# Linear attention with routed experts on one core: the last steps in another order, and the last head of the last block projected by rows

## The reference, cut to what matters

```python
qkv = silu(xn @ w_qkv.T); q, k, v = split per head            # 16 heads of 128
# per head, by blocks of rows, with a state kv that decays:
o_inter = (q * q_decay) @ kv
o_intra = ((q @ k.T) * diag_decay) @ v
kv = block_decay * kv + (k * k_decay).T @ v
out = o_inter + o_intra                                        # all heads side by side: 2048 columns
var = mean(out * out, axis=-1)
out = norm_w * (out * rsqrt(var + EPS))
gate = sigmoid(xn @ w_gate.T)
attn = (gate * out) @ w_out.T                                  # back to 256 columns
result = x + attn + (routed experts + shared experts)(xn)
```

## Time and profile before

| | |
|---|---|
| median of 3 runs | 1753.86 us (1752.04 to 1755.01) |
| the profiled execution | 1752.27 us, its span 1750.5 us |
| granted TensorE clock, mean | 0.997 of full speed |
| TensorE busy | 1709.8 us (98%), weight loads 1513.5 us |
| VectorE busy | 1308.6 us (75%) |
| ScalarE, GpSimd busy | 720.2 us, 607.3 us |

### The profile page before, as it was taken

The page is one execution under the profiler, slowest core; times in us unless marked ns, Lnnn a source line. Parts: engine busy times, 40 slices in busy tenths (PEclk is TensorE's granted clock), DMA queues, the critical chain, the costliest instruction groups (busy, mean ns, idle before and its releaser), DMA issues.

```text
span 1750.5 us, 34484 instructions
## 1 busy us (share of the span) xinstructions
PE 1709.8 (98%) x11705; PEld 1513.5 (86%) x11705; DVE 1308.6 (75%) x2590; ACT 720.2 (41%) x1331; POOL 607.3 (35%) x826
## 2 busy tenths in 40 slices
PE   6999999999999999999999999999999999999997
PEld 5888899899988888888888888889999999999996
DVE  7888788888776676666667667668888888876666
ACT  4333443434344444444444444443434343434331
POOL 2333155555343333433333343333333323210011
PEclk9999999999999999999999999999999999999998
DMA  6666444344478888878888787854444444331234
GB/s 219 217 218 232 139 137 150 129 147 134 151 235 255 243 247 251 247 243 245 251 249 249 244 256 238 256 170 134 124 125 125 129 117 139 103 113 51 78 99 133
DMA packets 283501, 316.02 MB, mean 181 GB/s; under 512 B 37696, under 2 KB 233280, under 8 KB 283328
## 3 DMA queue, kind: packets, MB, share of 16 engines
q1 hardware_dynamic: 211008, 175.34, 32.7%
q0 software_dynamic: 33792, 88.13, 16.7%
q10 hardware_dynamic: 38528, 50.34, 8.1%
HBM read 169.21 MB, written 144.46 MB: 179 GB/s over the span
## 4 chain that ended last, share of the span: by engine, by line
PE 73%; DMA 12%; DVE 5%; POOL 4%; issue 4%; ACT 1%; SPq 0%; DVEq 0%; ACTq 0%; POOLq 0%
DMA rows_turned<-xz 12%; PE bank L1251 6%; PE bank L1293 6%; PE bank L1252 6%; PE bank L1253 6%; PE bank L1276 5%; PE bank L1231 5%; PE bank L1233 5%; PE bank L1232 5%; PE bank L1296 5%; PE bank L1284 5%; POOL xsT L582 4%; PE bank L1307 3%; PE bank L1305 3%; PE bank L1306 3%
## 5 line engine op out<-in xcount | busy, mean ns | idle before, releaser
L582 POOL DMA_DIRECT2D xsT<-rows_turned x384 | 210.3, 554 | 388.4 <-DMA rows_turned<-xz 378.3
L1251 PE MATMUL bank<-wh,xh 128*128 128x256 f32 x1024 | 293.9, 287 | 0.0
L1253 PE MATMUL bank<-wh,xl 128*128 128x256 f32 x1024 | 289.1, 282 | 0.0
L1252 PE MATMUL bank<-wl,xh 128*128 128x256 f32 x1024 | 288.9, 282 | 0.0
L680 ACT ACTIVATE kv<-bank 128x512 f32<-128x512 f32 x256 | 153.1, 598 | 224.4 <-PE bank L1253 224.4
L593 POOL DMA_INDIRECT yk<-slot_y,pos x128 | 131.7, 1029 | 260.5 <-DVE xr L1005 171.2
L1039 DVE STREAM_TRANSPOSE kz<-kv 128x512 f32<-128x512 f32 x127 | 90.2, 710 | 166.0 <-issue 149.0
L1251 PEld LDWEIGHTS bank<-wh,xh 128*128 128x128 f32 x1024 | 193.3, 189 | 19.2 <-issue 15.9
L1231 PE MATMUL bank<-xh,wh 128*128 128x512 f32 x512 | 208.9, 408 | 0.0
L1055 DVE SCALAR_TENSOR_TENSOR og<-tg,bank 128x512 f32<-128x512 f32 x128 | 88.0, 687 | 155.0 <-ACT o L706 155.0
L1293 PE MATMUL bank<-sm,kv 128*128 128x128 f32 x1024 | 197.9, 280 | 4.7 <-DVE sm L1019 4.4
(11 more groups left out here) (165 smaller groups left out, 3692.2 us busy)
## 6 DMA issues: line engine op xcount, KB each, us to landing
keys_turned<-kz SPq DMA_DIRECT2D x127, 256.0 KB, 2.9
kT_by_group<-keys_turned SPq DMA_DIRECT2D x508, 64.0 KB
slot_x<-zeros ACTq DMA_DIRECT2D x8, 3072.0 KB, 10.2
xs<-slot_x SPq DMA_DIRECT2D x96, 256.0 KB, 3.8
we<-wexp_in SPq DMA_DIRECT2D x192, 128.0 KB, 3.0
rows_turned<-xz POOLq DMA_DIRECT2D x96, 256.0 KB, 4.1
xsT<-rows_turned POOLq DMA_DIRECT2D x384, 64.0 KB, 3.0
slot_y<-ys ACTq DMA_DIRECT2D x96, 256.0 KB, 3.9
```

Of the source, the lines that this page charges most:

```text
L582: pool.dma_start(xsT[q % 2][b * TB:(b + 1) * TB, :, :, :].rearrange("p a k j -> p a (k j)"), xz_back[q % 2, b]).then_inc(xsT_loaded[q % 2] ...
L1251: pe.matmul(dst, lh, rh, start=(k == 0), stop=False)
L1252: pe.matmul(dst, lh, rl, start=False, stop=False)
L1253: mm = pe.matmul(dst, ll, rh, start=False, stop=(k == KD - 1))
```

## The change

- **Turns 122 to 127.** `squares` moves from the end of the turn to before `project_out(s-2, 1)`. `turn_back` moves up to the end of the same turn, before the next turn's keys' and values' projection. `last_sum` moves to the start of the next turn on VectorE, and `mean_squares` ahead of `low_og`.
- **After the loop.** The loops of TensorE and VectorE end at turn 127 and the rest is written out (SyncE's loop ends one turn earlier). `scores(127)` stands ahead of `project_out(126, 0)`. `project_out(126, 1)` writes bank 2, so that it needs not wait for the first half to be added. `squares(6)` goes to bank 3, `squares(7)` to bank 5.
- **Last block, last head.** `earlier_heads` turns block 7's `acc` as it stands after 15 heads, by fp32 matmuls against the identity, into banks 0 and 1, open for accumulation. `last_head` adds the last head's projection there, with `ogh` and `ogl` as the stationary operand, 256 output features wide: 12 matmuls of 128x256. `add_out(127, ...)` is gone.
- **Last step's gate.** `gate_o(127)` waits for bank 4 alone; ScalarE makes `ogh` first and squares afterwards.
- **Stores.** There are three `res` buffers in place of two (with their semaphores), and each block is stored in two halves of 256 KB, the first after two of the four sums.

```diff
@@ -447,26 +448,27 @@
             def load_last(b):
-                if b < 2:
+                if b < 3:
                     for r in range(2):
...
                 else:
-                    sp.wait_ge(out_stored[b % 2], 16 * (b // 2))
-                sp.dma_start(res[b % 2][:], part2_grp[b]).then_inc(res_loaded[b % 2], 16)
+                    sp.wait_ge(out_stored[b % 3], 32 * (b // 3))
+                sp.dma_start(res[b % 3][:], part2_grp[b]).then_inc(res_loaded[b % 3], 16)
...
             def store_last(b):
-                sp.wait_ge(final, CH * (b + 1))
-                sp.dma_start(out_grp[b], res[b % 2][:]).then_inc(out_stored[b % 2], 16)
+                for h in range(0, CH, 2):
+                    sp.wait_ge(final, CH * b + h + 2)
+                    sp.dma_start(out_grp[b][:, h:h + 2, :], res[b % 3][:, h:h + 2, :]).then_inc(out_stored[b % 3], 16)
...
                 load_head(1, part)
-            for s in range(SLOTS + 1):
+            for s in range(SLOTS):
                 q0 = 2 * (s - EXPERT0)
...
                     pair_done(q0 - 1)
-                if s > FIRST_OUT + 3:
-                    store_last(s - FIRST_OUT - 4)
+                if s > FIRST_OUT + 2:
+                    store_last(s - FIRST_OUT - 3)
                 if s == EXPERT0 - 2:
@@ -493,12 +495,12 @@
                 if s == FIRST_OUT:
-                    for b in range(2):
+                    for b in range(3):
                         load_last(b)
-                if FIRST_OUT + 4 <= s < FIRST_OUT + 2 + NSB:
-                    load_last(s - FIRST_OUT - 2)
-            for r in range(2):
-                sp.wait_ge(out_stored[r], 16 * NSB // 2)
+                if FIRST_OUT + 4 <= s < FIRST_OUT + 1 + NSB:
+                    load_last(s - FIRST_OUT - 1)
+            for r in range(3):
+                sp.wait_ge(out_stored[r], 32 * len(range(r, NSB, 3)))
@@ -702,6 +704,8 @@
                 act.wait_ge(o_mm, j + 1)
+                if j == NSTEP - 1:
+                    act.wait_ge(og_ready, j + 1)
                 act.wait_ge(ssq_added, j)
@@ -750,7 +754,10 @@
                     silu_pair(q0 + 1)
-                if attends:
+                if s == NSTEP:
+                    high_og(s - 1)
+                    square_o(s - 1)
+                elif attends:
                     square_o(s - 1)
@@ -1051,7 +1058,9 @@
                 dve.wait_ge(tanh_done, j + 1)
-                dve.wait_ge(o2_ready, j + 1)
+                dve.wait_ge(o_mm, j + 1)
+                if j < NSTEP - 1:
+                    dve.wait_ge(o2_ready, j + 1)
                 dve.scalar_tensor_tensor(og[:], tg[:], 1.0, bank[4][:], ALU.add, ALU.mult).then_inc(og_ready, 1)
@@ -1061,11 +1070,12 @@
                 a = acc[:, k, tok(d % NSB)]
+                src = bank[2 if (d, k) == (NSTEP - 2, 1) else 5][:]
                 if d < NSB:
-                    dve.tensor_copy(a, bank[5][:]).then_inc(acc_added, 1)
+                    dve.tensor_copy(a, src).then_inc(acc_added, 1)
                 else:
                     dve.wait_ge(acc_added, KD * (d - NSB) + k + 1)
-                    dve.tensor_tensor(a, a, bank[5][:], ALU.add).then_inc(acc_added, 1)
+                    dve.tensor_tensor(a, a, src, ALU.add).then_inc(acc_added, 1)
@@ -1080,19 +1090,23 @@
                 dve.wait_ge(rms_mm, b + 1)
-                dve.tensor_scalar(rmsv[:, b * CH:(b + 1) * CH], bank[6][:, 0:CH], 1.0 / (NH * HD), RMS_EPS,
+                src = bank[(3, 5)[b - NSB + 2] if b >= NSB - 2 else 6][:, 0:CH]
+                dve.tensor_scalar(rmsv[:, b * CH:(b + 1) * CH], src, 1.0 / (NH * HD), RMS_EPS,
                                   ALU.mult, ALU.add).then_inc(rmsv_ready, 1)
...
             def last_sum(b):
-                dve.wait_ge(accT_mm, b + 1)
+                if b < NSB - 1:
+                    dve.wait_ge(accT_mm, b + 1)
                 dve.wait_ge(rms_ready, b + 1)
-                dve.wait_ge(res_loaded[b % 2], 16 * (b // 2 + 1))
-                for c in range(CH):
-                    o = res[b % 2][:, c, :]
-                    src = bank[6 + c // 2][:, (c % 2) * D:(c % 2 + 1) * D]
+                dve.wait_ge(res_loaded[b % 3], 16 * (b // 3 + 1))
+                for c in range(CH):
+                    o = res[b % 3][:, c, :]
+                    if b == NSB - 1:
+                        dve.wait_ge(last_mm, c // 2 + 1)
+                    src = bank[(0 if b == NSB - 1 else 6) + c // 2][:, (c % 2) * D:(c % 2 + 1) * D]
                     dve.scalar_tensor_tensor(o, src, rms[:, b * CH + c:b * CH + c + 1], o, ALU.mult, ALU.add).then_inc(final, 1)
...
-            for s in range(SLOTS):
+            for s in range(NSTEP):
                 experts = EXPERT0 <= s < EXPERT1
@@ -1100,6 +1114,8 @@
                     add_squares(s - 2)
+                if s > FIRST_OUT + 2:
+                    last_sum(s - FIRST_OUT - 3)
                 if EXPERT0 <= s + 1 < EXPERT1:
@@ -1129,20 +1145,31 @@
                     decay_queries(s)
-                if s > FIRST_OUT + 2:
-                    last_sum(s - FIRST_OUT - 3)
                 if experts:
...
                     add_out(s - 2, 1)
+                if s >= FIRST_OUT + 2:
+                    mean_squares(s - FIRST_OUT - 2)
                 if attends:
...
                     routing(0)
-                if FIRST_OUT + 2 <= s < SLOTS - 1:
-                    mean_squares(s - FIRST_OUT - 2)
+            update_state(NSTEP - 1)
+            decay_scores(NSTEP - 1)
+            add_squares(NSTEP - 2)
+            last_sum(NSB - 3)
+            gate_o(NSTEP - 1)
+            add_out(NSTEP - 2, 0)
+            low_og(NSTEP - 1)
+            add_squares(NSTEP - 1)
+            add_out(NSTEP - 2, 1)
+            mean_squares(NSB - 2)
+            mean_squares(NSB - 1)
+            last_sum(NSB - 2)
+            last_sum(NSB - 1)
@@ -1299,12 +1326,13 @@
                 pe.wait_ge(ogl_ready, d + 1)
-                pe.wait_ge(acc_added, KD * d + f)
+                pe.wait_ge(acc_added, KD * d + (f if d < NSTEP - 2 else 0))
                 cols_ = slice(WC + f * P, WC + (f + 1) * P)
                 lh, ll = wh[h % 2][:, cols_], wl[h % 2][:, cols_]
-                pe.matmul(bank[5][:], lh, ogh[:], start=True, stop=False)
-                pe.matmul(bank[5][:], lh, ogl[:], start=False, stop=False)
-                pe.matmul(bank[5][:], ll, ogh[:], start=False, stop=True).then_inc(out_mm, 1)
+                dst = bank[2 if (d, f) == (NSTEP - 2, 1) else 5][:]
+                pe.matmul(dst, lh, ogh[:], start=True, stop=False)
+                pe.matmul(dst, lh, ogl[:], start=False, stop=False)
+                pe.matmul(dst, ll, ogh[:], start=False, stop=True).then_inc(out_mm, 1)
@@ -1338,14 +1366,43 @@
                 pe.wait_ge(ssq_added, FIRST_OUT + b + 1)
+                if b < NSB - 2:
+                    pe.wait_ge(final, CH * b)
+                elif b == NSB - 2:
+                    pe.wait_ge(state_step, updates_before(NSTEP - 1, CH - 1))
+                else:
+                    pe.wait_ge(acc_added, KD * (NSTEP - 2) + 1)
+                dst = bank[(3, 5)[b - NSB + 2] if b >= NSB - 2 else 6][:, 0:CH]
+                for c in range(CH):
+                    t = b * CH + c
+                    mm = pe.matmul(dst[:, c:c + 1], ssq[:, t * P:(t + 1) * P], ones[:], start=True, stop=True)
+                mm.then_inc(rms_mm, 1)
+
+            def earlier_heads():
+                pe.wait_ge(q_silu, NSTEP)
+                pe.wait_ge(tanh_done, NSTEP)
+                pe.wait_ge(acc_added, KD * (NSTEP - NSB))
+                for c in range(CH):
+                    t = (NSB - 1) * CH + c
+                    for k in range(KD):
+                        o = (c % 2) * D + k * P
+                        pe.matmul(bank[c // 2][:, o:o + P], acc[:, k, t * P:(t + 1) * P], ident[:], start=(c % 2 == 0 and k == 0), stop=False)
+
+            def last_head():
+                pe.wait_ge(ogl_ready, NSTEP)
+                h = NH - 1
+                rh, rl = wh[h % 2][:, WC:WC + D], wl[h % 2][:, WC:WC + D]
+                for c in range(CH):
+                    dst = bank[c // 2][:, (c % 2) * D:(c % 2 + 1) * D]
+                    pe.matmul(dst, ogh[:, ch[c]], rh, start=False, stop=False)
+                    pe.matmul(dst, ogl[:, ch[c]], rh, start=False, stop=False)
+                    mm = pe.matmul(dst, ogh[:, ch[c]], rl, start=False, stop=(c % 2 == 1))
+                    if c % 2:
+                        mm.then_inc(last_mm, 1)
+
+            def turn_back(b):
+                pe.wait_ge(rmsv_ready, min(b + 1, NSB - 2))
                 pe.wait_ge(final, CH * b)
-                for c in range(CH):
-                    t = b * CH + c
-                    mm = pe.matmul(bank[6][:, c:c + 1], ssq[:, t * P:(t + 1) * P], ones[:], start=True, stop=True)
-                mm.then_inc(rms_mm, 1)
-
-            def turn_back(b):
-                pe.wait_ge(rmsv_ready, b + 1)
```

(27 more changed lines are left out.)

2 lines of the change are left out of this document (1 added, 1 removed).

## The result

The changed kernel took 1747.93 us, the median of 6 runs (1745.86 to 1749.13), the kernel before 1753.01 beside it. The ratio is 0.9969, with a 95% interval of 0.9956 to 0.9981: faster by 5.1 us. Forecast were 1747.4 us and -6.5. Two executions, one of the kernel before (1873 us, clock 0.85) and one of the later many_waits (3147 us, clock 0.83), fell into a much slower state and are left out everywhere.

A forecast was written before the change was run, and what follows sets the result against it. TensorE was taken to bound the loop, leaving only the tail to win: 0 in the loop, -5.74 to the sums' end, -0.77 in the store, so -6.5 from the median 1753.86 to 1747.4 us; range 1745.0 to 1750.6.

The forecast's parts named there:

- The bound, and where the gain lies: TensorE, busy 1709.8 of 1750.5 us, bounds the loop; turns 122 to 127 win nothing, all gain lies in the tail.
- Turn 128: First turn behind the loop: attention of step 127 starts 0.82 us earlier, `og` 1.32 us earlier.
- Behind it: TensorE after that turn's attention: fp32 turning of block 7 takes 1.78 us; block 6's transposes complete at 1737.95, root at 1738.0.
- VectorE's end: The last sums, of blocks 6 and 7, end at 1741.35 instead of 1747.09: -5.74 us.
- The store: Last store, at the span's end, halved from 512 KB: -0.77 us, bounds +0.4 to -0.8.
- The sum: Whole kernel: 0 in the loop, -5.74 to the end of the sums, -0.77 in the store: -6.5 us.
- Its own sign of being wrong: Wrong if VectorE waits before the sum of block 7, or the span shrinks by less than 5 or more than 8 us.
- Rival 1: The clock falls in the new tail, costing 2.2 at most or 5.0 if earlier; middle 2.5, so 1749.9 us; chance 0.13.
- Rival 2: The tail is shortened, but other waits at thin margins take half of it: 1750.7 us; chance 0.10.
- Rival 3: `turn_back` waits at the end of each of turns 122 to 127, making it slower: 1759.4 us; chance 0.03.

The follow-up runs named there:

- many_waits: The kernel before with five more waits ahead of VectorE's gate in each of the 128 steps; ratio 1.0002, end 94.64 us.
- filled: The kernel before with 12 dummy matmuls of 128x512 put where TensorE waits in the last turns; end 93.94 us.
- by_transposes: The changed kernel, but the 15 heads' sum of block 7 is turned by eight transposes instead of fp32 matmuls; end 89.74 us.
- again: The changed kernel once more, unaltered; end 89.39 us, ratio 0.9975.
- last_wait: The changed kernel, but VectorE's gate waits for the attention's matmuls only in the last step; ratio 0.9969, end 89.37 us.
- through_acc: The changed kernel, but block 7's last head goes the old way: two projections, two additions into acc, eight transposes after them; end 91.10 us.
- reordered: The changed kernel with turning by transposes, the gate's added wait only in the last step, and the end in another order; 1745.09 us, ratio 0.9949.

## Why the prediction was right

- **The bound, and where the gain lies.** Right. The two turns of the earlier trace rows cost what they did, and all of the gain came from behind the loop and one wait of 0.36 us. That the edits cost nothing in the loop was off by the 0.2 us of the added wait, which the prediction does not mention.
- **Turn 128.** Attention was to start 0.82 us earlier, and `og` 1.32. Counted from the tanh of step 121 they start 0.92 (77.24 against 76.32) and 1.56 earlier (80.04 against 78.48). The rest is the overlap on VectorE: I added up durations of 0.68, but the next instruction starts 0.60 after the last.
- **Behind it.** The fp32 turning was put at 1.78 and issued for 1.87 us (1736.20 to 1738.07). The root took 1.01 us, not 1.39, and the transposes alone held the sum of block 6; the two were not 0.05 apart but about 0.5. With 1.39 the root would still have been 0.2 us early.
- **VectorE's end.** -5.74 forecast, -6.14 measured (92.86 against 86.72). Right in its steps, too small by the overlaps. But the -5.74 counts a tail that ran in part at 1.2 GHz as if it always did. Against many_waits, whose sums end at 91.22, it is -4.5: which course of the clock the one profile had was luck.
- **The store.** -0.77 forecast, -0.72 measured in the end (3.41 against 2.69 us behind the last sum), and 0.78 undone by itself. The Trainium skill, "DMA: Bandwidth & Descriptors", gives the formula that the prediction sets beside this for DMAs that GpSimd issues; these stores are issued by SyncE, and the whole one landed in 2.9 us and the half in 2.2, against 3.2 and 2.6 as estimates by the formula.
- **The sum.** -6.5 against -6.86 or -5.2 at the end. The median moved by 5.1. Undone one by one, the parts are worth 1.7 (projection by rows), 0.8 (store), 0.6 (scores), 0.4 (gate) and 0.3 (turns), together 3.7 us. At full clock on both sides (filled against the changed kernel) the end is 4.5 us shorter. So some 0.8 us are left for the order of squares and mean squares and for the second bank, which no run undoes by themselves, and the clock has the other 0.7 to 2.3.
- **Its own sign of being wrong.** It names a span that shrinks by less than 5 us, and the span shrank by 4.6 (1750.5 to 1745.9). 2.26 us were lost ahead of the tanh of step 121; of them 1.6 us were lost before the loop's first tanh (199.95 against 198.34), after a fall of the clock that both kinds of kernel have in some executions (last paragraph of this section).
- **Rival 1, the clock.** It did not fall in the changed kernel. What I had not said is that of the gain 0.7 to 2.3 us comes from the clock falling in the kernel before. In by_transposes it fell inside the transposes of block 6 and made them 0.64 us longer, about half of the 1.1 that the rival has for a fall ahead of them.
- **Rival 2, thin margins.** Not met. `ssq` was in time: the second squares follow the turning without a wait. The keys were copied 0.20 us before the scores. One margin was read too wide: the load of block 7's `res` took 5.2 us to land (1735.37 to 1740.58) and 5.7 in again, not 3.9, and was 1.0 and 0.5 us ahead of its sum, not 2.
- **Rival 3, a wait in each turn.** Not met; 0.43 us to spare in turn 127 where I had 0.3 (0.20 up to the weight load).

**What stays open.** All 28 timed executions of the changed kernel and of last_wait have a mean of 1748.5 us, 43 of the kernel before one of 1753.4. That is 4.9 less. The end explains 5.2 to 6.9 of gain, by the course of the clock in the kernel before, so between 0.3 and 2 us are lost ahead of it, or chance does that for all these runs. Two small parts are known. The added wait costs 0.2 us in the first 28 turns. And in three of the 14 profiles, of both kinds of kernel (after, through_acc and many_waits), the clock fell near 35 us, in the first phase; these reach the loop's first tanh at 199.6 to 200.1 us, the others at 198.0 to 198.8. The window from 36 to 38 in the profile after has a clock of 0.50:

```profile
36.00:38.00 2.00, 2.00 (x11) 2.00 (x11) 1.90 (x3) 0.00 (x0) 0.00 (x0) 0.50 1.03 373
```

Most of the spread is in the 48 turns with the experts, 28 to 75 (the description of the kernel has 28 to 92, and an expectation 64 turns; `EXPERT1` is `EXPERT0` + 48). They wait for DMAs and took 677.3 to 682.7 us in the ten profiles that have the new end, with a mean of 680.1, and 678.1 to 679.8 in the four with the old. No run of mine tells chance there from a cause. reordered, with the same turns as last_wait, ran 8.2 us faster than before where its end accounts for 6.2 to 7.8.

## What to carry to other kernels

In a kernel that one engine bounds, add up its tail separately: order is free in the loop and costs every wait behind it. A product that is needed turned can be made turned, by swapping which operand is stationary, and accumulated onto the turned sum of what is there already; that takes an addition and a transposition out of the chain. To judge a change of a few microseconds, measure from the last instruction ahead of it: in three profiles of the changed kernel's tail that stretch repeated to 0.04 us, where whole runs spread over 8. But take more than one profile of each side: the old tail came out 1.6 us apart in two, because the clock fell at another place.

## What the runs showed that I had not expected

- One order of instructions has more than one course of the clock. With the same squares and the same wait of 1.45 us the clock fell in the kernel before and stayed up in many_waits, and it stayed up in through_acc with waits of 1.40 and 0.87 us, but fell in by_transposes, whose longest wait in the last 4 us before was 0.47. The length of a wait alone does not tell whether it falls.
- An fp32 transpose can open an accumulation that fp32r matmuls then add to: eight took 1.07 us, where eight fp32 matmuls by the identity took 2.03.
- GpSimd's power of 128x4 has two durations, and what VectorE does beside it goes with them. In the 14 profiles it took 1.38 to 1.46 us in all 88 cases in which VectorE's `add_squares` or `low_og` ran beside it (both inputs in tiles, none in a bank) and 1.01 in all 24 in which neither did, also beside `last_sum`, which reads a bank. The root of block 6 fits: 1.39 before, with `add_squares` right behind `mean_squares`, and 1.01 in the changed kernel. No run changes this alone, so the cause is argued from the rows.
